# One turn of the second layer's loop for one pair of groups: scores, maximum, weighting and carries together

## The chip, the cores and the metric

The kernel runs on 1 core of one Trainium2 chip. The metric is the device time of that core in microseconds. TensorE (PE) multiplies, VectorE (DVE), ScalarE (ACT) and GpSimd (POOL) do the rest, SyncE (SP) issues most plain DMAs.

## The reference

Two graph layers run over 3125 nodes with 256 features and 50000 edges sorted by destination. The first layer is an edge network (two tanh layers, a gate from the edge attributes, a mean over the senders). The change is in the second one, an attention layer with 4 heads of 64 features:

```python
h = einsum('ni,hio->hno', x, W)
e = attn_src[:, src] + attn_dst[:, dst]
e = where(e >= 0, e, 0.2 * e) * edge_weight
e_exp = exp(e - max(e))
denom = segment_sum(e_exp, dst)
alpha = e_exp / (denom[dst] + 1e-10)
out = segment_sum(h[src] * alpha, dst)
x = layernorm(x + out)
```

## The kernel before, in words

The edges are cut into 391 blocks of 128 edges, 98 groups of 4 blocks and 49 pairs of groups (`NQ`, counted by `q`; the last pair has 7 blocks). The program first makes tables for the first layer, runs the edge network over the 98 groups (to about 1.6 ms), normalises, and writes `HT`, a table in DRAM with 260 numbers a node: the 256 features of the 4 heads and the 4 source scores. Then the second layer runs over the edges in order of destination:

- **POOL** (L1419 to L1423) gathers the rows of `HT` for each block with one indirect DMA (issue at L1407) into the ring `Hg`, which holds 12 groups (`HGR`). A group's slots are used again when VectorE has weighted the group 12 before it (`s_xb`).
- **SP** (L1300 to L1306) brings, for each pair, the destinations' remainders by broadcast into `rem` (2 slots), and stores each finished window `hist` (6 slots) to `HB` in DRAM.
- **VectorE** makes for each pair the matrix `hot` (`one_hot`, L897) and the matrices `in_window` (`window_rows`, L906). `edge_scores(q)` waits for the gathered rows of the pair and for TensorE's products of destination scores, then runs five short instructions one behind the other: add (L921), slope (L929), weight (L935), largest (L938), and the diagonal matrix `diag` of the largest (L943). `running_maximum(q)` (L950, L954) waits for TensorE's spread of that diagonal and lowers `neg_m`. `weighted_rows(g)` (L959 through `weigh`) waits for ScalarE's exponentials and writes `xb`, the rows by their weights. `carry_window(g)` (L978, L990) waits for TensorE's sums of the group and adds the window of the group before.
- **TensorE** runs `destination_scores(q)` (24 small products, L1678), `spread_maxima(q)` (L1687), and `window_sums(g)` (4 products, each recorded as two, L1698). It takes these in program order.
- **ScalarE** (L1942 to L1955) makes `drop` and the two exponentials (L1951, L1953) of a pair as soon as `neg_m` is there.

What each waits for is told by semaphores written by hand. One of them crosses from VectorE to TensorE each turn: `destination_scores(q)` waits for `s_sc` to reach `3 * (q - 1) + 1`, the first instruction of `edge_scores(q - 1)`, since both use the bank `PAD`.

The order in which VectorE takes the steps is a loop written out by hand (L1009 to L1030). It is staggered over pairs: turn `q` weights and sums pair `q`, carries pair `q - 1`, takes the maximum of pair `q + 1`, the scores of pair `q + 2`, and makes `hot` of pair `q + 3`. TensorE's loop (L1704 to L1712) has the same stagger. Every seventh pair VectorE also makes the next 14 groups' destination scores (`window_scores`, L882 to L889, six times in the loop), and once the tables for the end (`last_rows`, L995 to L1006). After the loop come `chosen` and `scale` (L1034, L1036), then the gather of the finished windows (L1473), the residual, the normalisation and the stores.

Of the kernel before, what the change touches and what calls it, by code (L numbers as in the profile page):

```python
# [17 lines left out]
def build_program(nc, xT, x, src_cols, dst_cols, src_row, dst_row, eT, w_cols,  # L18
# [85 lines left out]
    with ctx:  # L104
# [446 lines left out]
        def _(dve):  # L551
# [339 lines left out]
            def one_hot(q):  # L891

                n = edges_of_group(2 * q) + edges_of_group(2 * q + 1)
                dve.wait_ge(s_rem[q % 2], 16 * (q // 2 + 1))
                if q >= 2:
                    dve.wait_ge(s_ad, q - 1)
                dve.tensor_scalar(hot[:, q % 2, 0:n], rem[:, q % 2, 0:n], p_f[:, :], None, ALU.is_equal).then_inc(s_hot, 1)  # L897
# [13 lines left out]
            def edge_scores(q):  # L911

                blocks = blocks_of_window_pair(q)
                runs = same_rows(blocks)
                dve.wait_ge(s_hg[2 * q % HGR], group_arrivals(HGR, 2 * q))
                dve.wait_ge(s_hg[(2 * q + 1) % HGR], group_arrivals(HGR, 2 * q + 1))
                dve.wait_ge(s_ad, q + 1)
                for run in runs:
                    n, b, k = rows_of_block(run[0]), run[0], len(run)
                    j, r = b - blocks[0], b % (HGR * BLOCKS_PER_GROUP)  # L920
                    last = dve.tensor_tensor(  # L921
                        score[0:n, b:b + k, :], Hg[0:n, r:r + k, OUT:BW],
                        PAD[0:n, j * HEADS:(j + k) * HEADS].rearrange("p (k h) -> p k h", h=HEADS), ALU.add)
                last.then_inc(s_sc, 1)
                dve.wait_ge(s_sc, 3 * q + 1)
                for run in runs:
                    n, b, k = rows_of_block(run[0]), run[0], len(run)
                    v = score[0:n, b:b + k, :]
                    last = dve.scalar_tensor_tensor(v, v, NEG_SLOPE, v, ALU.mult, ALU.max)  # L929
                last.then_inc(s_sc, 1)  # L930
                dve.wait_ge(s_sc, 3 * q + 2)
                for run in runs:
                    n, b, k = rows_of_block(run[0]), run[0], len(run)
                    v = score[0:n, b:b + k, :]
                    last = dve.tensor_tensor(v, v, w_c[0:n, b:b + k].unsqueeze(2).to_broadcast([n, k, HEADS]), ALU.mult)  # L935
                last.then_inc(s_sc, 1)
                dve.wait_ge(s_sc, 3 * q + 3)
                dve.tensor_reduce(top_c[:, q:q + 1], score[:, blocks[0]:blocks[-1] + 1, :].rearrange("p b h -> p (b h)"),  # L938
                                  AX.X, ALU.max).then_inc(s_topc, 1)
                dve.wait_ge(s_topc, 2 * q + 1)  # L940
                if q >= 2:
                    dve.wait_ge(s_sp, q - 1)
                dve.tensor_scalar(diag[:, q % 2, :], ident[:, :], top_c[:, q:q + 1], None, ALU.mult).then_inc(s_topc, 1)  # L943

            def running_maximum(q):

                dve.wait_ge(s_sp, q + 1)
                if q >= 2:
                    dve.wait_ge(s_nm, q - 1)
                dve.tensor_reduce(top_g[:, q % 2:q % 2 + 1], PTOP[:, 0:P], AX.X, ALU.max).then_inc(s_mg, 1)  # L950
                dve.wait_ge(s_mg, q + 1)
                if q >= 1:
                    dve.wait_ge(s_nm, q)
                dve.scalar_tensor_tensor(neg_m[:, q + 1:q + 2], top_g[:, q % 2:q % 2 + 1], -1.0, neg_m[:, q:q + 1],  # L954
                                         ALU.mult, ALU.min).then_inc(s_nm, 1)
# [7 lines left out]
            def weighted_rows(g):  # L963

                dve.wait_ge(s_ex, g // 2 + 1)
                for run in same_rows(blocks_of_group(g)):
                    n, b, k = rows_of_block(run[0]), run[0], len(run)
                    j, i = b % (XBR * BLOCKS_PER_GROUP), b % (2 * BLOCKS_PER_GROUP)
                    r = b % (HGR * BLOCKS_PER_GROUP)
                    last = weigh(xb[0:n, j:j + k, 0:OUT], Hg[0:n, r:r + k, 0:OUT], weight_p(g // 2)[0:n, i:i + k], n, k)  # L970
                last.then_inc(s_xb, 1)

            def carry_window(g):

                q = g // 2
                if g % 2 == 0:
                    dve.wait_ge(s_drop, q + 1)
                    dve.tensor_tensor(drop_k[:, q:q + 1], drop[:, q:q + 1], keep[:, g:g + 1], ALU.mult).then_inc(s_dk, 1)  # L978
                dve.wait_ge(s_S, g + 1)
                if g >= HISTR:  # L980
                    dve.wait_ge(s_hd[g % HISTR], 16 * (g // HISTR))
                if g == 0:
                    dve.tensor_copy(hist[:, 0, 0:BW], PS[0][:, 0:BW]).then_inc(s_carry, 1)
                    return
                carried = keep[:, g:g + 1]
                if g % 2 == 0:
                    dve.wait_ge(s_dk, q + 1)
                    carried = drop_k[:, q:q + 1]
                dve.wait_ge(s_carry, g)
                dve.scalar_tensor_tensor(hist[:, g % HISTR, 0:BW], hist[:, (g - 1) % HISTR, 0:BW], carried,  # L990
                                         PS[g % 3][:, 0:BW], ALU.mult, ALU.add).then_inc(s_carry, 1)
# [14 lines left out]
                const(dve.tensor_copy(last_g[:, :, NG - 1:NG], reached[:, :, NG - 1:NG]), "last")  # L1006

            window_scores(0)
            for q in range(-3, NQ + 1):  # L1009
                if 0 <= q < NQ:  # L1010
                    weighted_rows(2 * q)
                if 0 <= q - 1:
                    carry_window(2 * q - 2)
                if 0 <= q + 1 < NQ:
                    running_maximum(q + 1)

                if 0 <= q + 2 < NQ:
                    edge_scores(q + 2)
                if 0 <= q < NQ:
                    weighted_rows(2 * q + 1)  # L1020
                if 0 <= q - 1:
                    carry_window(2 * q - 1)
                if q + 3 < NQ:
                    one_hot(q + 3)
                if 0 <= q + 1 < NQ:
                    window_rows(q + 1)
                if q >= 0 and 2 * q % ADC == 2 and 2 * q // ADC + 1 < NG // ADC:
                    window_scores(2 * q // ADC + 1)
                if q == ADC // 4:
                    last_rows()  # L1030
# [141 lines left out]
        def _(sp):  # L1172
# [121 lines left out]
            def load_remainders(q):  # L1294
                a, n = 2 * q * GE, min(2 * GE, E - 2 * q * GE)
                if q >= 2:
                    sp.wait_ge(s_hot, q - 1)
                sp.dma_start(rem[:, q % 2, 0:n], RD[0, a:a + n].partition_broadcast(P)).then_inc(s_rem[q % 2], 16)

            for q in range(-5, NQ):  # L1300
                if q + 5 < NQ:
                    load_remainders(q + 5)
                if q >= 0:
                    for g in (2 * q, 2 * q + 1):
                        sp.wait_ge(s_carry, g + 1)
                        sp.dma_start(HB[g * P:(g + 1) * P, :], hist[:, g % HISTR, :]).then_inc(s_hd[g % HISTR], 16)  # L1306
# [172 lines left out]
        def _(pe):  # L1479
# [202 lines left out]
            def spread_maxima(q):  # L1682

                pe.wait_ge(s_topc, 2 * q + 2)
                if q >= 1:
                    pe.wait_ge(s_mg, q)
                pe.matmul(PTOP[:, 0:P], ones[:, :], diag[:, q % 2, :], start=True, stop=True).then_inc(s_sp, 1)  # L1687

            def window_sums(g):

                pe.wait_ge(s_win, g // 2 + 1)
                pe.wait_ge(s_xb, g + 1)
                if g >= 3:
                    pe.wait_ge(s_carry, g - 2)
                blocks = blocks_of_group(g)
                for b in blocks:
                    n, j = rows_of_block(b), b % (XBR * BLOCKS_PER_GROUP)
                    last = pe.matmul(PS[g % 3][:, 0:BW], in_window[0:n, j, :], xb[0:n, j, :],  # L1698
                                     start=b == blocks[0], stop=b == blocks[-1])
                last.then_inc(s_S, 1)  # L1700

            pe.wait_ge(s_hc, NT)
            pe.wait_ge(s_x1c, NT)
            for q in range(-3, NQ):  # L1704
                if q >= 0:
                    window_sums(2 * q)
                if 0 <= q + 2 < NQ:
                    spread_maxima(q + 2)
                if q >= 0:
                    window_sums(2 * q + 1)  # L1710
                if q + 3 < NQ:
                    destination_scores(q + 3)  # L1712

            with if_outside(pe):
                pe.wait_ge(s_b2, B2["ones"])
# [330 lines left out]
```

## Time and profile before

| | us |
|---|---|
| median of 3 runs | 2242.31 (2242.23 to 2244.2) |
| span of the profiled execution | 2239.4 |
| start of the second layer's gathers | 1672.5 |
| first instruction of the second layer's first scores | 1684.28 |
| first instruction behind the loop (`chosen`) | 2185.59 |

The profiled execution's own time is given only by its span, which is 2.9 us under the median of the runs; that difference is what lies around the span.

Busy shares of the span: PE 87%, DVE 68%, ACT 62%, POOL 66%. In the second layer they are lower, and there the granted clock of TensorE moves between its two levels.

How to read the rows: times are microseconds from the span's start. A line of the timeline has the start, the duration, the engine, the line of the kernel and the operation with output and input; in brackets is how long the engine had been idle and what released it. A line of the groups has the busy time, the mean duration of one in ns, and behind the bar the idle time before them. Matmuls in a timeline are merged where they follow one another.

### The profile page before, as it was taken

To read this page: it belongs to the slowest core of one execution; us is meant where nothing else is said; L and a number is where in the kernel's file an instruction comes from. 1 tells how busy PE (TensorE), PEld (TensorE's weight loads), DVE (VectorE), ACT (ScalarE), POOL (GpSimd) and SP (SyncE) were. 2 spreads that over 40 slices of the span, in tenths; PEclk is the share of its full clock that TensorE was granted. 3 is DMA by queue.
4 is the path that set the end of the run, shared out by engine and by line. 5 is a ranking of instruction groups with operands and counts; after the bars stand their busy time and mean duration, and the time that the engine had idled before them with its cause. 6 is when DMAs were issued, how large, how long until landed. Compare 5 with 4: busy or idle time off the path is not lost.

```text
span 2239.4 us, 40504 instructions
## 1 busy us (share of the span) xinstructions
PE 1938.9 (87%) x12932; PEld 1717.4 (77%) x12932; DVE 1513.0 (68%) x3765; ACT 1377.2 (62%) x2758; POOL 1488.4 (66%) x1229
## 2 busy tenths in 40 slices
PE   7799999999999999999999999999664676666660
PEld 6699999999999999999999999999653455445450
DVE  6566676676666766766666667666565766666667
ACT  3488888888888888888888888888550000000012
POOL 0427677777777677777776767775427777777754
PEclk9899999999999999999999999999886767877785
DMA  7988877777777777776777777776555566656544
GB/s 241 297 221 188 201 167 171 165 161 172 158 168 171 149 167 159 154 167 152 159 165 149 166 159 154 167 153 129 119 183 142 148 160 158 161 154 162 155 125 128
DMA packets 233059, 370.78 MB, mean 166 GB/s; under 512 B 32743, under 2 KB 165825, under 8 KB 232839
## 3 DMA queue, kind: packets, MB, share of 16 engines
q0 software_dynamic: 101232, 188.20, 42.2%
q1 hardware_dynamic: 131607, 179.89, 27.5%
q8 instruction: 108, 1.77, 0.3%
q14 instruction: 112, 0.92, 0.1%
HBM read 270.57 MB, written 97.40 MB: 164 GB/s over the span
## 4 chain that ended last, share of the span: by engine, by line
PE 70%; POOL 14%; DMA 6%; issue 5%; DVE 4%; ACT 1%; SPq 0%; DVEq 0%; ACTq 0%; POOLq 0%
PE bank L1483 16%; PE bank L1482 16%; PE bank L1484 16%; POOL Hg L1407 13%; PE bank L1536 5%; PE bank L1527 5%; PE bank L1553 3%; DMA Hg<-HT,src_c 3%; PE bank L1577 2%; PE bank L1578 2%; PE bank L1589 2%; PE bank L1588 2%; DMA accA<-ystage,to_a 1%; PE bank L1654 1%; DVE xb L959 1%
## 5 line engine op out<-in xcount | busy, mean ns | idle before, releaser
L1369 POOL DMA_INDIRECT accA<-ystage,to_a x391 | 653.6, 1672 | 244.0 <-DMA accA<-ystage,to_a 113.9
L1375 POOL DMA_INDIRECT GA<-TA,src_c x391 | 424.9, 1087 | 292.7 <-issue 95.4
L1407 POOL DMA_INDIRECT Hg<-HT,src_c x391 | 378.3, 968 | 121.1 <-issue 112.8
L1482 PE MATMUL bank<-h1h,W1h 128*128 128x512 f32 x882 | 348.4, 395 | 0.0
L1484 PE MATMUL bank<-h1h,W1l 128*128 128x512 f32 x882 | 347.5, 394 | 0.0
L1483 PE MATMUL bank<-h1l,W1h 128*128 128x512 f32 x882 | 347.5, 394 | 0.0
L563 DVE TENSOR_TENSOR h2l<-h2f,h2h 128x512 fp32r<-128x512 f32 (+1 forms) x294 | 203.1, 691 | 200.8 <-ACT h2l L1769 130.5
L1698 PE MATMUL bank<-xb,in_window 128*128 128x260 f32 (+1 forms) x782 | 273.1, 509 | 58.6 <-issue 56.9
L1944 ACT ACTIVATE drop<-neg_m 128x1 f32<-128x1 f32 x49 | 14.4, 295 | 455.0 <-DVE neg_m L954 455.0
L563 DVE TENSOR_TENSOR h1l<-h1f,h1h 128x512 fp32r<-128x512 f32 x294 | 195.1, 691 | 129.5 <-ACT h1h L1769 129.5
L1698 PEld LDWEIGHTS bank<-xb,in_window 128*128 128x128 f32 (+1 forms) x782 | 190.4, 256 | 103.9 <-issue 68.4
L1769 ACT ACTIVATE mh<-mf 128x512 fp32r<-128x512 f32 x196 | 124.3, 634 | 227.5 <-DVE mf L717 227.5
L1483 PE MATMUL bank<-W2l,h2h 128*128 128x256 f32 (+1 forms) x782 | 220.5, 282 | 0.0
L1482 PE MATMUL bank<-W2h,h2h 128*128 128x256 f32 (+1 forms) x782 | 219.7, 281 | 0.4 <-DVE mf L717 0.4
L1484 PE MATMUL bank<-W2h,h2l 128*128 128x256 f32 (+1 forms) x782 | 219.9, 281 | 0.0
L1806 ACT ACTIVATE h1f<-bank 128x512 f32<-128x512 f32 (+1 forms) x392 | 206.8, 584 | 1.0 <-DVE stB L563 0.8
L1831 ACT ACTIVATE h2f<-bank,b1c 128x512 f32<-128x512 f32 x294 | 201.9, 687 | 6.7 <-PE bank L1553 1.7
L1484 PEld LDWEIGHTS bank<-h1h,W1l 128*128 128x128 f32 x882 | 166.4, 189 | 39.1
L717 DVE TENSOR_TENSOR mf<-bank,gate 128x512 f32<-128x512 f32 x196 | 135.3, 690 | 84.1 <-PE bank L1578 84.1
L1769 ACT ACTIVATE h2h<-h2f 128x512 fp32r<-128x512 f32 x294 | 185.4, 631 | 9.4
L1482 PEld LDWEIGHTS bank<-h1h,W1h 128*128 128x128 f32 x882 | 166.4, 189 | 32.1 <-issue 0.2
L1483 PEld LDWEIGHTS bank<-h1l,W1h 128*128 128x128 f32 x882 | 166.5, 189 | 30.2
(217 smaller groups left out, 4819.2 us busy)
## 6 DMA issues: line engine op xcount, KB each, us to landing
TW<-TB SPq DMA_DIRECT2D x196, 203.0 KB, 3.5
ef<-in_eT SPq DMA_DIRECT2D x97, 256.0 KB, 4.6
bcast_i<-in_src_row SPq DMA_DIRECT2D x97, 256.0 KB, 5.6
HB<-hist SPq DMA_DIRECT2D x98, 130.0 KB, 3.1
rel<-RL SPq DMA_DIRECT2D x97, 128.0 KB, 5.6
rem<-RD SPq DMA_DIRECT2D x48, 256.0 KB, 4.6
TB<-stB SPq DMA_DIRECT2D x24, 406.0 KB, 4.5
accA<-zeros SPq DMA_DIRECT2D x4, 1677.0 KB, 13.7
```

Of the source, the lines that this page charges most:

```text
L563: return dve.tensor_tensor(o, full, hi.bitcast(f32), ALU.subtract)
L717: dve.tensor_tensor(mf[0:n, q % 2, 0:k, :].rearrange("p i d -> p (i d)"), P2[0:n, 0:k * OUT], gate[0:n, q % 2, 0:k, :].rearrange("p i d -> ...
L1369: return pool.indirect_dma_start(out=table, out_offset=bass.IndirectOffsetOnAxis(ap=rows, axis=0), in_=sums, in_offset=None, compute_op=AL ...
L1375: pool.indirect_dma_start(out=GA[0:n, b % (GAR * BLOCKS_PER_GROUP), :].bitcast(f32), out_offset=None, in_=TA, in_offset=bass.IndirectOffse ...
L1407: pool.indirect_dma_start(out=Hg[0:n, slot, :], out_offset=None, in_=HT, in_offset=bass.IndirectOffsetOnAxis(ap=src_c[0:n, b:b + 1], axis= ...
L1482: pe.matmul(o, lh, rh, start=first, stop=False)
L1483: pe.matmul(o, lh, rl, start=False, stop=False)
L1484: return pe.matmul(o, ll, rh, start=False, stop=last)
L1698: last = pe.matmul(PS[g % 3][:, 0:BW], in_window[0:n, j, :], xb[0:n, j, :], start=b == blocks[0], stop=b == blocks[-1])
L1769: return act.activation(o, i, ACT.Copy)
L1806: act.activation(h1f[0:k1(c), c, 0:n], PT[u % 2][0:k1(c), 0:n], ACT.Tanh).then_inc(s_tanh1, 1)
L1831: act.activation(h2f[:, m, 0:n], PL1[u % 2][:, 0:n], ACT.Tanh, bias=b1c[:, m:m + 1]).then_inc(s_tanh2, 1)
```

## The change

VectorE's loop, SP's loop over the remainders and TensorE's loop are rewritten so that turn `q` does `edge_scores`, `running_maximum`, `weighted_rows` and `carry_window` of the same pair `q`. `one_hot(q + 2)` stands between the scores and the maximum, `window_rows(q + 1)` between the maximum and the weighting. The work inside each helper is unchanged, and no buffer changes its size.

```diff
             window_scores(0)
-            for q in range(-3, NQ + 1):
-                if 0 <= q < NQ:
-                    weighted_rows(2 * q)
-                if 0 <= q - 1:
-                    carry_window(2 * q - 2)
-                if 0 <= q + 1 < NQ:
-                    running_maximum(q + 1)
-
-                if 0 <= q + 2 < NQ:
-                    edge_scores(q + 2)
-                if 0 <= q < NQ:
-                    weighted_rows(2 * q + 1)
-                if 0 <= q - 1:
-                    carry_window(2 * q - 1)
-                if q + 3 < NQ:
-                    one_hot(q + 3)
-                if 0 <= q + 1 < NQ:
+            one_hot(0)
+            one_hot(1)
+            window_rows(0)
+            for q in range(NQ):
+                edge_scores(q)
+                if q + 2 < NQ:
+                    one_hot(q + 2)
+                running_maximum(q)
+                if q + 1 < NQ:
                     window_rows(q + 1)
-                if q >= 0 and 2 * q % ADC == 2 and 2 * q // ADC + 1 < NG // ADC:
+                weighted_rows(2 * q)
+                weighted_rows(2 * q + 1)
+                carry_window(2 * q)
+                carry_window(2 * q + 1)
+                if 2 * q % ADC == 2 and 2 * q // ADC + 1 < NG // ADC:
                     window_scores(2 * q // ADC + 1)
                 if q == ADC // 4:
                     last_rows()
...
-            for q in range(-5, NQ):
-                if q + 5 < NQ:
-                    load_remainders(q + 5)
+            for q in range(-4, NQ):
+                if q + 4 < NQ:
+                    load_remainders(q + 4)
...
-            for q in range(-3, NQ):
-                if q >= 0:
-                    window_sums(2 * q)
-                if 0 <= q + 2 < NQ:
-                    spread_maxima(q + 2)
-                if q >= 0:
-                    window_sums(2 * q + 1)
-                if q + 3 < NQ:
-                    destination_scores(q + 3)
+            destination_scores(0)
+            for q in range(NQ):
+                if q + 1 < NQ:
+                    destination_scores(q + 1)
+                spread_maxima(q)
+                window_sums(2 * q)
+                window_sums(2 * q + 1)
```

## Rows read from the trace of the kernel before

**Rows 1.** Busy time of each engine in one stretch, the second layer's loop.

```profile
core 0: us, PE busy (x) PEld busy (x) DVE busy (x) ACT busy (x) POOL busy (x), PEclk, DMA share, GB/s
1685.00:2186.00 501.00, 323.72 (x2029) 246.77 (x2029) 334.06 (x735) 38.73 (x153) 368.71 (x381) 0.77 0.60 152
```

**Rows 2.** Costliest groups of the page: the gathers and the window sums.

```profile
L1407 POOL DMA_INDIRECT Hg<-HT,src_c x391 | 378.3, 968 | 121.1 <-issue 112.8
L1698 PE MATMUL bank<-xb,in_window 128*128 128x260 f32 (+1 forms) x782 | 273.1, 509 | 58.6 <-issue 56.9
```

**Rows 3.** Line L1407 alone: shortest, median, longest in ns, first and last start.

```profile
L1407 POOL DMA_INDIRECT Hg<-HT,src_c x391: 902/953/3446, 1672.5 to 2168.8; - x196
```

**Rows 4.** Groups by line from 1715 us on: VectorE's wait for the gathered rows.

```profile
L921 DVE TENSOR_TENSOR score<-Hg,bank 128x32 f32<-128x32 f32 x44 | 8.3, 188 | 125.9 <-DMA Hg<-HT,src_c 125.9
```

**Rows 5.** Timeline at the start of the loop: scores and maximum of pair 0.

```profile
1684.28 0.19 DVE L921 TENSOR_TENSOR score<-Hg,bank 128x32 f32<-128x32 f32 x1 [8.65 <-DMA Hg<-HT,src_c]
...
1685.17 0.29 DVE L943 TENSOR_SCALAR diag<-ident,top_c 128x128 f32<-128x128 f32 x1
...
1685.51 0.80 PE L1687 MATMUL bank<-diag,ones 128*128 128x128 f32 x2 [8.85 <-DVE diag L943]
...
1686.35 0.29 DVE L950 TENSOR_REDUCE top_g<-bank 128x1 f32<-128x128 f32 x1 [0.49 <-PE bank L1687]
```

**Rows 6.** Timeline: TensorE's spread and destination scores, both at the full clock.

```profile
1973.51 0.49 PE L1687 MATMUL bank<-diag,ones 128*128 128x128 f32 x2 [4.17 <-DVE diag L943]
...
2158.58 0.87 PEld L1678 LDWEIGHTS bank<-ad_p,hot 128*128 128x128 bf16 x24
```

**Rows 7.** Timeline of one turn from weighting on, 1961.7 to 1969.4 us.

```profile
1961.71 1.21 DVE L959 TENSOR_TENSOR xb<-Hg,bank 128x1024 f32<-128x1024 f32 x1
...
1963.03 3.80 PE L1698 MATMUL bank<-xb,in_window 128*128 128x260 f32 x8 [0.38 <-issue]
...
1963.63 1.22 DVE L906 TENSOR_TENSOR in_window<-bank,rem_c 128x1024 f32<-128x1024 f32 x1
...
1964.77 1.21 DVE L959 TENSOR_TENSOR xb<-Hg,bank 128x1024 f32<-128x1024 f32 x1
...
1966.26 0.48 DVE L990 SCALAR_TENSOR_TENSOR hist<-hist,drop_k,bank 128x260 f32<-128x260 f32 x1 [0.21 <-DVE drop_k L978]
...
1966.66 0.28 DVE L950 TENSOR_REDUCE top_g<-bank 128x1 f32<-128x128 f32 x1
...
1966.98 0.16 DVE L954 SCALAR_TENSOR_TENSOR neg_m<-top_g,neg_m 128x1 f32<-128x1 f32 x1
...
1967.31 2.03 PE L1698 MATMUL bank<-xb,in_window 128*128 128x260 f32 x8
...
1967.59 0.30 ACT L1953 ACTIVATE xb<-score,neg_m 128x32 f32<-128x32 f32 x1
```

**Rows 8.** Timeline: the two window sums of two other turns.

```profile
1952.70 2.81 PE L1698 MATMUL bank<-xb,in_window 128*128 128x260 f32 x8 [0.68 <-issue]
...
1955.98 2.56 PE L1698 MATMUL bank<-xb,in_window 128*128 128x260 f32 x8
...
2155.46 3.50 PE L1698 MATMUL bank<-xb,in_window 128*128 128x260 f32 x8 [0.68 <-issue]
...
2159.41 2.00 PE L1698 MATMUL bank<-xb,in_window 128*128 128x260 f32 x8
```

**Rows 9.** Timeline: first instruction of `window_scores` and `last_rows`, and the one behind.

```profile
1718.88 1.60 DVE L882 TENSOR_TENSOR picked<-bank,in_tile 128x1400 f32<-128x1400 f32 x1
...
1722.99 1.21 DVE L959 TENSOR_TENSOR xb<-Hg,bank 128x1024 f32<-128x1024 f32 x1
...
1740.12 0.40 DVE L995 TENSOR_SCALAR n_f<-tile_row,p_f 128x25 f32<-128x25 f32 x1
...
1749.09 1.22 DVE L959 TENSOR_TENSOR xb<-Hg,bank 128x1024 f32<-128x1024 f32 x1
```

**Rows 10.** Timeline of the loop's end: the last pair's scores and the work behind.

```profile
2171.72 0.24 DVE L921 TENSOR_TENSOR score<-Hg,bank 128x24 f32<-128x24 f32 x2 [1.86 <-DMA Hg<-HT,src_c]
...
2185.59 2.71 DVE L1034 TENSOR_TENSOR chosen<-last_g,factor 128x2450 f32<-128x2450 bf16 x1
```

## The prediction, as put on record

> **What bounds the kernel now.** The change touches only the second layer's loop, so I read the busy times of that stretch first [rows 1]: in 501 us no engine is full. POOL has 369 us, DVE 334, PE 324, ACT 39. A bound must then be a pace or a chain. The groups say which: POOL's 391 gathers have 968 ns each and lose almost nothing but "issue" between them [rows 2], so POOL runs from the first to the last without a pause that another engine causes. They start from 1672.5 to 2168.8 us [rows 3]: 496.3 us for 390 steps, 1.273 us a gather, 10.2 us for a pair of 8. DVE on its side waits 125.9 us for gathered rows in the adds that open the scores [rows 4]. So **the gathers set the pace, at 10.2 us a pair, and DVE and PE have slack in every turn**. The stagger over pairs makes that slack: scores of one pair, weighting of another and carries of a third lie side by side. Behind the last landing it costs a tail: from the last pair's add at 2171.72 to `chosen` at 2185.59 is 13.9 us [rows 10].
>
> **What the change removes and adds.** No instruction is added or dropped, only the order changes. Before, DVE's results were needed one or two steps later. Now each turn is one closed chain through three engines: DVE scores, PE spread, DVE maximum, DVE weighting, PE sums of two groups, DVE carries. The next scores stand behind the last carry in DVE's order. I add the chain up from the first add (time 0).
>
> 1. From the add to `diag` are 0.89 us, and the spread can start 0.34 later [rows 5], at 1.23. But PE now has the destination scores of pair q+1 ahead of the spread, and these wait for the add of pair q (0.19 us, plus the 0.1 us that PE needs behind DVE, below): from 0.3 they take 0.87 us of weight loads [rows 6] and about 0.1 behind them, to 1.3. So the spread starts at 1.3, an extra 0.1 us. The new `one_hot(q + 2)` costs nothing: DVE would wait for the spread here in any case. Without that cover it would be about 0.4 us.
> 2. The spread takes 0.49 us at the full clock [rows 6] or 0.80 at the half [rows 5], and DVE's reduce follows 0.04 us behind (1685.51 + 0.80 to 1686.35) [rows 5]. It starts at 1.8 to 2.3; I take 2.0.
> 3. From the reduce to `neg_m` is 0.32 us, and `neg_m` takes 0.16 [rows 7]; with the step to the next instruction 0.52. `window_rows(q + 1)` stands here for 1.14 us (1963.63 to 1964.77) [rows 7]. It hides ScalarE: the second exponential ends 0.91 us behind the start of `neg_m` (1966.98 to 1967.89) [rows 7], so without it the weighting would start only some 0.4 us earlier. The first weighting takes 1.21 and PE starts 0.11 behind it (1962.92 to 1963.03) [rows 7]. PE's sums start at 2.0 + 0.52 + 1.14 + 1.21 + 0.11 = 5.0 us (4.8 at the full clock). The second weighting ends before the first sums do, so it is hidden.
> 4. **The two sums** lie back to back. This is the term with wide bounds. A group takes 2.03 us at the full clock and 3.80 at the half [rows 7], so the two take 4.0 to 7.6 us. The mean of all is 273.1 us over 98 groups, 2.79 each [rows 2], or 5.58 for two. The new order brings a break in PE's heavy work of 5.4 us in each turn, with only the scores and the spread in it. In the rows of before the sums that open a burst took 3.80, 2.81 and 3.50 us, the ones that came 3.3 to 4.3 us after that start took 2.03, 2.56 and 2.00 [rows 7, 8]. Now the second group starts when the first ends, so the clock has risen less often by then. I take 3.4 for the first and the mean 2.8 for the second, 6.2 us.
> 5. The last carry starts 0.04 us behind the sums (as the reduce behind the spread) and the next instruction 0.40 later (1966.26 to 1966.66) [rows 7]: 0.44. The first carry lies beside the second group's sums and is hidden.
>
> A turn is 5.0 + 6.2 + 0.44 = 11.6 us, against the gathers' 10.2. **DVE's chain becomes the bound**, and what was hidden in its slack is paid in full: six `window_scores` of 4.1 us (1718.88 to 1722.99) and one `last_rows` of 9.0 (1740.12 to 1749.09) [rows 9], 33.7 us.
>
> **Moved and free.** The opening `one_hot(0)`, `one_hot(1)` and `window_rows(0)` lie in the 8.65 us that DVE waits for the first rows [rows 5]. SP's load of remainders runs four pairs ahead instead of five, behind the carries of the turn before; it has about two turns until its matrix is wanted, and if that cover failed DVE would stand in `one_hot` with the maximum queued behind it. POOL's ring is freed sooner in relation to the scores (one pair is in use, not three), so the gathers run ahead and then wait for `xb`; DVE should no longer wait for rows at all. The stores of windows and everything from `chosen` on keep their order behind the last carry: zero.
>
> **The sum.** First add 1684.28, since the first landing is unchanged [rows 5]. 49 turns of 11.6 are 568.4, plus 33.7: the loop ends at 2286.4. Before, `chosen` started at 2185.59 [rows 10]. The difference is +100.8 us in the profiled execution, whose span is 2239.4: a span of 2340.2. The runs' median stands 2.9 us over the span, so **2343 us** (+4.5%).
>
> What the Trainium skill says on step 4: its page "TensorE: Matmul & The Clock Gate", section "HAM oscillation — how this bites in real kernels", tells of kernels whose bursts of products, parted by waits, start at the half clock every time. The trace agrees in part: the openers above were slow or in between, the followers mostly fast. Taken strictly, with both groups slow, it makes the second rival below.
>
> **The rivals.**
> - *The gathers stay the bound.* If PE kept the full clock, a turn would be 4.8 + 4.06 + 0.44 = 9.3 us. 49 such turns and 33.7 end at 2173.7, before the last rows could be worked off: they land at 2171.7, and one turn behind is 2181.0, 4.6 us earlier than now. That gives 2238 us, faster. For it: the tail does shrink. Against: the granted clock of the stretch is 0.77 already [rows 1] and PE's breaks grow. The point from which it decides is a turn of 9.5 us: (2185.6 - 1684.3 - 33.7) / 49. Chance 4%.
> - *Every sum at the half clock.* A turn is 5.3 + 7.6 + 0.44 = 13.3 us: 651.7 + 33.7 ends at 2369.7, +184, so 2426 us. For it: the breaks come in every turn. Against: the groups that follow an opener were mostly fast in the rows [rows 7, 8]. Chance 6%.
> - *A turn between 9.5 and 10.5 us*, with waits that overlap in a way I don't see, gives 2242 to 2290. Chance 4%, of which 1% falls within 0.2% of now.
>
> That the change does not do what it says I give no chance: each engine takes its list in order, and the waits in the chain are data.
>
> **How the numbers follow.** The forecast has 86%. Its own spread comes from step 4 and from the spread's clock: two sums of 5.3 us (under the mean of now) give a turn of 10.7 and 2299, two of 7.1 give 12.5 and 2387. The range of 2300 to 2385 leaves out about 2 in 10 with the rivals. Everything but the first rival and a corner of the third is slower by over 0.2% (4.5 us, about what a measurement of this kernel can tell from no change): faster 4%, same 1%, slower 95%.
>
> **What would show it.** Right: the scores' add no longer waits for `Hg`; POOL waits for `xb` instead and its time from first to last gather grows to nearly 600 us; the carry (L990) waits for L1698 some 4 to 6 us a turn, and PE for `diag` or `xb`; adds follow each other at 11 to 12 us. Step 1 is right if the spread starts behind the last destination product. Step 4 is wrong if the mean of L1698 falls towards 2.03 us a group or rises over 3.5. The whole is wrong if DVE still waits for gathered rows in most turns: then the gathers still bound it.

## The result

The changed kernel takes 2298.1 us (median of 4 runs, 2297.22 to 2301.32) against 2242.3 for the kernel before: a ratio of 1.025, with a 95% interval of 1.0235 to 1.0264. It is slower, as forecast, by 55.8 us where 100.8 were forecast. The range began 2 us above the measured time (2300), so the forecast was wrong in size.

The chain that ended last, from the pages of the two kernels, before and after. The first one is followed back through the whole span, the second through the second layer only (its shares add up to 25%), so PE's shares can't be compared. What can be read is that POOL, 14% of the span before, has left the chain, and PE and DVE hold it:

```profile
PE 70%; POOL 14%; DMA 6%; issue 5%; DVE 4%; ACT 1%; SPq 0%; DVEq 0%; ACTq 0%; POOLq 0%
...
PE 13%; DVE 8%; issue 4%; POOL 0%; ACT 0%; DMA 0%; ACTq 0%; DVEq 0%
```

The costliest groups, against [rows 2]. The lines have moved: the gathers are at L1403, the window sums at L1694.

```profile
L1403 POOL DMA_INDIRECT Hg<-HT,src_c x391 | 377.5, 966 | 137.1 <-issue 113.9
L1694 PE MATMUL bank<-xb,in_window 128*128 128x260 f32 (+1 forms) x782 | 273.5, 524 | 142.7 <-issue 135.7
```

The window sums cost what they cost before (273.5 us against 273.1), but PE now stands idle 142.7 us ahead of them instead of 58.6. The gathers by their own line, against [rows 3]:

```profile
L1403 POOL DMA_INDIRECT Hg<-HT,src_c x391: 902/957/3455, 1672.2 to 2183.7; - x196
...
  DVE xb L959: 20.9, 16
...
  DVE score L921: 6.8, 1
```

The second line shown is how long POOL waited for a slot of the ring (20.9 us), the third who waited for the gathers: one add, the first. Against 125.9 us in [rows 4], **VectorE waits for no gathered row any more**. Where it waits instead is in the list of waits from 1715 to 2225 us (waiting line, released by, total, times, longest):

```profile
DVE hist L990 <- PE bank L1694: 181.1, 90, 2.7
...
PE bank L1674 <- DVE score L921: 64.5, 45, 9.6
POOL Hg L1403 <- DVE xb L959: 20.9, 16, 5.3
...
DVE top_g L950 <- PE bank L1683: 10.1, 39, 0.6
```

The carries wait 181 us for the window sums, and the destination scores on PE wait for the scores' add, which stands behind those carries. One settled turn, in the timeline:

```profile
2212.39 0.18 DVE L921 TENSOR_TENSOR score<-Hg,bank 128x32 f32<-128x32 f32 x1
...
2213.28 0.28 DVE L943 TENSOR_SCALAR diag<-ident,top_c 128x128 f32<-128x128 f32 x1
...
2213.62 0.49 PE L1683 MATMUL bank<-diag,ones 128*128 128x128 f32 x2 [0.16 <-DVE diag L943]
...
2214.48 0.16 DVE L954 SCALAR_TENSOR_TENSOR neg_m<-top_g,neg_m 128x1 f32<-128x1 f32 x1
...
2215.69 2.34 DVE L959 TENSOR_TENSOR xb<-Hg,bank 128x1024 f32<-128x1024 f32 x2
...
2217.00 5.20 PE L1694 MATMUL bank<-xb,in_window 128*128 128x260 f32 x16 [2.89 <-issue]
...
2220.48 0.48 DVE L990 SCALAR_TENSOR_TENSOR hist<-hist,drop_k,bank 128x260 f32<-128x260 f32 x1 [2.39 <-PE bank L1694]
...
2222.24 0.48 DVE L990 SCALAR_TENSOR_TENSOR hist<-hist,keep,bank 128x260 f32<-128x260 f32 x1 [1.27 <-PE bank L1694]
...
2222.64 0.18 DVE L921 TENSOR_TENSOR score<-Hg,bank 128x32 f32<-128x32 f32 x1
```

The reader is to see one closed chain of 10.25 us: 4.61 from the add to the sums, 3.48 for the first sum and 1.76 from it to the second, 0.40 from the last carry to the next add. The first sum is slow and the second fast. The loop's ends, against [rows 5] and [rows 10]:

```profile
1684.01 0.19 DVE L921 TENSOR_TENSOR score<-Hg,bank 128x32 f32<-128x32 f32 x1 [6.83 <-DMA Hg<-HT,src_c]
...
2244.49 2.70 DVE L1030 TENSOR_TENSOR chosen<-last_g,factor 128x2450 f32<-128x2450 bf16 x1
```

The start is where it was and the end is 58.9 us later, which is the whole difference of the spans (2297.2 against 2239.4) but for 1.1 us. With the 33.7 us of side work (`window_scores` and `last_rows`) taken off, 49 turns took (560.5 - 33.7) / 49 = 10.75 us each.

The mean is longer than the settled turn, and the difference is most of what the chain itself costs. A turn behind side work takes 11.4 to 11.9 us: its first sum takes 3.8 us, and the second is partly slow as well (2.3 to 2.8 us behind the first). The turns behind it take 10.8, 10.5, 10.4 us and so on, down to 10.25. Had all 49 turns been settled, they would have taken 49 x 10.25 = 502 us, and the whole loop took 501.3 us before. So the settled turn as such costs nothing. The 59 us are the side work, 33.7 us, and about 24 us of turns that had not settled, the first and the last of the loop among them.

### The profile page after: what moved, and what is told of

Read it like the earlier page. It is cut to its first block and busy times, and to the rows that moved or that the text cites. A ratio compares the mean times of both kernels' runs of the same rounds, so it can differ in the third digit from the quotient of the medians.

```text
span 2297.2 us, 40504 instructions
## 1 busy us (share of the span) xinstructions
PE 1953.1 (85%) x12932; PEld 1730.3 (75%) x12932; DVE 1518.3 (66%) x3765; ACT 1378.1 (60%) x2758; POOL 1490.6 (65%) x1229
## 5 line engine op out<-in xcount | busy, mean ns | idle before, releaser
L1403 POOL DMA_INDIRECT Hg<-HT,src_c x391 | 377.5, 966 | 137.1 <-issue 113.9
L1694 PE MATMUL bank<-xb,in_window 128*128 128x260 f32 (+1 forms) x782 | 273.5, 524 | 142.7 <-issue 135.7
L1694 PEld LDWEIGHTS bank<-xb,in_window 128*128 128x128 f32 (+1 forms) x782 | 208.3, 274 | 197.8 <-issue 151.4
```

The source lines that it names most:

```text
L1403: pool.indirect_dma_start(out=Hg[0:n, slot, :], out_offset=None, in_=HT, in_offset=bass.IndirectOffsetOnAxis(ap=src_c[0:n, b:b + 1], axis= ...
```

## The experiments

Theory A: in the new order scores, spread, maximum, weighting, sums and carries are one chain through three engines, closed because the next scores stand behind the last carry, and its widest term is a first window sum that meets TensorE at the half clock. The rival: the clock, or the order, has no part in it, and either the gathers still set the pace or the chain is long whatever is moved. The runs went to several chips. On two of them the kernel before itself takes 2400.7 and 2398.6 us and not 2241, and the traces taken there show VectorE in waits for TensorE that the other chips don't show. So of the runs on these slower chips only what stands in single turns is used, and all of them but the first below were made again on another chip.

**Fewer gathers in the changed kernel** (on a slower chip).

```diff
-                for b in blocks_of_group(g):
+                for b in blocks_of_group(g)[::1 if g < HGR else 2]:
                     gather_h_rows(b, b % (HGR * BLOCKS_PER_GROUP), s_hg[g % HGR])
```

(with the count of landings that VectorE waits for cut to match).

> The changed kernel, with only every second block of a group gathered from the 13th group on (the other blocks use the rows that an earlier group left in the ring, so the second layer's sums are of other rows). POOL's pace falls from 10.2 to about 5.1 us a pair. Theory A (the gathers no longer bound the changed kernel): within 5 us of 2298. Theory B (they still set the pace): 2220 us or less.

2360.7 us. The total does not answer: in the first turn VectorE stood 21.8, 16.7 and 15.0 us in waits for TensorE, which put 60.9 us between the first two adds. The turns behind it, in which no such wait is left, do. Here is the timeline of one near the end:

```profile
2243.53 0.18 DVE L921 TENSOR_TENSOR score<-Hg,bank 128x32 f32<-128x32 f32 x1
...
2248.13 5.21 PE L1694 MATMUL bank<-xb,in_window 128*128 128x260 f32 x16 [2.88 <-issue]
...
2251.63 0.48 DVE L990 SCALAR_TENSOR_TENSOR hist<-hist,drop_k,bank 128x260 f32<-128x260 f32 x1 [2.40 <-PE bank L1694]
...
2253.78 0.18 DVE L921 TENSOR_TENSOR score<-Hg,bank 128x32 f32<-128x32 f32 x1
```

10.25 us, to the hundredth what the changed kernel takes with all its gathers. All 48 turns behind the first took 544.0 us, against 548.2 in the changed kernel (from the second add to `chosen`). The gathers do not bound it.

**Fewer gathers in the kernel before**, by the same edit.

> The kernel before, with only every second block of a group gathered from the 13th group on (the other blocks use rows that an earlier group left in the ring, so the second layer's sums are of other rows). POOL's pace falls from 10.2 to 5.1 us a pair. Theory A (before, the gathers set the pace and VectorE and TensorE had slack): the loop falls to VectorE's and TensorE's own pace in the staggered order, about 8 to 8.5 us a turn, and the time to 2130 to 2190 us. Theory B (another chain was at 10 us a turn as well): 2235 us or more.

2113.8 us, ratio 0.944 (0.9424 to 0.9455): 127 us less, more than theory A had guessed. Busy times of the stretch 1760 to 1990 us (PE, PEld, DVE, ACT, POOL, then the granted clock):

```profile
1760.00:1990.00 230.00, 171.11 (x1351) 134.75 (x1350) 216.42 (x480) 23.00 (x96) 125.79 (x132) 0.93 0.61 151
```

VectorE is busy 216 of 230 us, and its adds follow each other at 6.5 us. So the staggered order needs 6.5 us a turn, and the gathers' 10.2 us hid 3.7 us in each. The new order needs 10.75 in the mean: 4.3 us more, of which the gathers' pace hides the first 3.7. What is left (0.55 us x 49 = 27 us, nearly all of it in turns that had not settled) and the side work, which had been hidden too (33.7), make the loss.

**Idle products ahead of the sums.**

```diff
                 spread_maxima(q)
+                for _ in range(8):
+                    pe.matmul(PAD[:, 2 * P:3 * P], ident[:, :], ident[:, :], start=True, stop=True)
                 window_sums(2 * q)
```

> The changed kernel with 8 idle products (identity by identity, 128x128, into unused columns of the bank of the destination scores) between the spread and the window sums, so that TensorE's break before the sums is filled. Theory A (the loop is one chain, and its widest term is the first window sum, which finds TensorE at the half clock: 3.66 us against 1.95 for the second): both sums take about 4.1 us together instead of 5.6, a turn about 9.1 us instead of 10.7; the gathers' pace of 10.2 us a pair binds again, and the time falls to 2238 to 2255 us. Theory B (the clock is no part of it, the chain is long by its steps alone): 2298 us or a little more, since the idle products can only delay the sums.

On a slower chip: 2496.0 us against 2400.7, no better than the changed kernel's other variants with all gathers there (2464 to 2491 us). Again, on another chip:

> The same kernel as e1_filler (8 idle products ahead of the window sums), since on the chip of the first four runs the kernel before took 2400.7 us and TensorE's semaphores reached VectorE some 4 us late once a turn. On a chip where the kernel before takes about 2242 us: theory A (the first window sum finds TensorE at the half clock, and that is the widest term of the chain) 2238 to 2255 us; theory B (the clock is no part of it) 2298 us or a little more.

2232.1 us, ratio to the kernel before 0.9967 (0.9955 to 0.9978): faster than both kernels, if by little over the kernel before (8.5 us), and 6 us below the 2238 to 2255 of theory A. The timeline of a settled turn, with the idle products at L1706:

```profile
1769.60 0.18 DVE L921 TENSOR_TENSOR score<-Hg,bank 128x32 f32<-128x32 f32 x1
...
1771.15 1.95 PE L1706 MATMUL bank<-ident 128*128 128x128 f32 x16
...
1774.20 3.75 PE L1694 MATMUL bank<-xb,in_window 128*128 128x260 f32 x16 [1.10 <-issue]
...
1776.23 0.48 DVE L990 SCALAR_TENSOR_TENSOR hist<-hist,drop_k,bank 128x260 f32<-128x260 f32 x1 [0.93 <-PE bank L1694]
...
1777.99 0.48 DVE L990 SCALAR_TENSOR_TENSOR hist<-hist,keep,bank 128x260 f32<-128x260 f32 x1 [1.27 <-PE bank L1694]
```

and the busy times of the loop but for its last 13 us, in the columns of [rows 1]:

```profile
1685.00:2165.00 480.00, 354.13 (x2741) 305.03 (x2741) 331.92 (x710) 35.81 (x145) 364.78 (x379) 0.90 0.61 157
```

The sums start 4.60 us behind the add, as in the changed kernel, since the idle products end 1.10 us before them. But both sums take 3.75 us here instead of 5.20, the granted clock of the loop is 0.90 instead of 0.77 (as read in the changed kernel too, 1685 to 2244 us), and a turn in which VectorE waits for no rows and does no side work is 8.8 us (from the add to 0.40 us behind the start of the last carry). VectorE waits for gathered rows again (21.3 us in 17 adds). Nothing was taken out of the kernel; work was added to TensorE, and 66 us went. So the half clock in the first sum was what kept the chain from lying under the gathers' pace: without it a turn leaves 1.4 us to pay for the side work.

**Idle products in the kernel before**, 4 ahead of each group's sums and behind the wait for the carry, which frees their bank.

```diff
     def window_sums(g):
-                pe.wait_ge(s_win, g // 2 + 1)
-                pe.wait_ge(s_xb, g + 1)
                 if g >= 3:
                     pe.wait_ge(s_carry, g - 2)
+                for _ in range(4):
+                    pe.matmul(PS[g % 3][:, 3 * P:4 * P], ident[:, :], ident[:, :], start=True, stop=True)
+                pe.wait_ge(s_win, g // 2 + 1)
+                pe.wait_ge(s_xb, g + 1)
```

> The kernel before with idle products too: 4 ahead of each group's window sums, as many in all as in e1_filler, into unused columns of the sums' own bank. Theory A (before, the gathers set the pace, so a faster TensorE brings nothing but a shorter end of the loop): within 4 us of the kernel before. Theory B (the gain of the idle products is their own, whatever the order of the loop): 8 us or more faster, as the changed kernel with them is.

On a slower chip 2433.1 against 2398.6, ratio 1.0138. Again, on another chip:

> The same kernel as e9_filler_before. Where the kernel before takes about 2241 us: theory A (the gathers set its pace, idle products bring at most a shorter end) within 4 us of it; theory B (the idle products' gain does not depend on the order of the loop) 8 us or more faster.

2241.1 us, ratio 1.0005 (0.9995 to 1.0015). No change, with the clock of the loop at 0.85: a faster TensorE brings nothing where the gathers set the pace. The gain above belongs to the closed chain.

**Side work ahead of the first carry.**

```diff
-                carry_window(2 * q)
-                carry_window(2 * q + 1)
                 if 2 * q % ADC == 2 and 2 * q // ADC + 1 < NG // ADC:
                     window_scores(2 * q // ADC + 1)
                 if q == ADC // 4:
                     last_rows()
+                carry_window(2 * q)
+                carry_window(2 * q + 1)
```

> The changed kernel with window_scores (six times 4.1 us) and last_rows (once 9.0 us) moved from behind the last carry of their turn to ahead of its first carry, where VectorE waits about 2.4 and 1.3 us for the window sums. Theory A (VectorE's chain is the bound, so what stands behind the last carry is paid in full): some 3.7 us of each of the seven is hidden, 26 us less, 2272 us; a few us more if the shorter breaks of TensorE also raise its clock. Theory B (something else sets the pace, the side work was hidden already): within 3 us of 2298.

On a slower chip: 2491.5 us. There the reduce of the maxima, not the side work, is what is late:

```profile
2000.90 0.49 PE L1683 MATMUL bank<-diag,ones 128*128 128x128 f32 x2 [0.16 <-issue]
...
2004.87 0.29 DVE L950 TENSOR_REDUCE top_g<-bank 128x1 f32<-128x128 f32 x1 [3.63 <-remote]
```

The spread ends at 2001.4 and VectorE starts 3.5 us later; in the kernel before, on another chip, that step is 0.04 us [rows 5]. What delays it is open. Again, on another chip:

> The same kernel as e2_side_work (window_scores and last_rows ahead of the first carry of their turn), for the same reason. Where the kernel before takes about 2242 us: theory A (VectorE's chain is the bound, work behind the last carry is paid in full) 2272 us, or a few us less; theory B (the side work was hidden already) within 3 us of 2298.

2267.5 us, ratio 1.0122 (1.0105 to 1.0139): 31 us less than the changed kernel. By the two traces the seven turns with side work are 3.3 to 3.9 us shorter each, 25 us in all, near the 26 of theory A. The rest lies mostly in the turns behind them: three are 0.4 to 1.5 us shorter, while the other four still take 11.4 to 11.6 us. The side work was paid in full, as step 5 and the paragraph behind it had it.

**The carries one turn later.**

```diff
+                if q >= 1:
+                    carry_window(2 * q - 2)
+                    carry_window(2 * q - 1)
                 running_maximum(q)
...
-                carry_window(2 * q)
-                carry_window(2 * q + 1)
...
+            carry_window(NG - 2)
+            carry_window(NG - 1)
```

> The changed kernel with one part undone: the two carries of pair q stand in turn q+1, between one_hot and the maximum, so VectorE starts the next pair's scores while TensorE still sums. Theory A (what closes the chain is that the scores of q+1 stand behind the carries of q): the turn becomes the two sums plus scores' products 0.95, spread 0.5, maximum 0.4, window_rows 1.1, weighting 1.2 and the steps between, 4.4 + 5.6 = 10.0 us or less, the side work is hidden beside the sums, and the gathers bind again: 2238 to 2255 us. Theory B (the chain through maximum, weighting and sums is long enough by itself): 2280 us or more.

On a slower chip: 2485.9 us. Again, on another chip:

> The same kernel as e3_carries_later (carries of pair q in turn q+1, between one_hot and the maximum), for the same reason. Where the kernel before takes about 2242 us: theory A (the scores of q+1 behind the carries of q close the chain) 2238 to 2255 us; theory B (maximum, weighting and sums are long enough by themselves) 2280 us or more.

2238.3 us, ratio 0.9989 (0.9979 to 0.9998). Moving the carries alone to the other side of the next scores gives all of the loss back. Most turns are 9.0 to 10.9 us and the clock of the loop is 0.76, so here the slow first sum stays and the gathers hide it. That it is the gathers is read from POOL: its gathers follow each other from 1672.6 to 2166.9 us with 2.1 us of waits for slots, as back to back as in the kernel before. VectorE waits 103.2 us ahead of the scores' adds; the profile names no releaser for it, but its only other wait there, for TensorE's products of destination scores, was over 4.9 us or more before each of these adds.

**`window_rows` in the wait for the sums** (moved from behind the maximum to behind the weighting).

```diff
                 running_maximum(q)
-                if q + 1 < NQ:
-                    window_rows(q + 1)
                 weighted_rows(2 * q)
                 weighted_rows(2 * q + 1)
+                if q + 1 < NQ:
+                    window_rows(q + 1)
```

> The changed kernel with window_rows(q + 1) moved from between maximum and weighting to behind the weighting, where VectorE waits for the sums. The weighting can start when the exponentials are there, 0.94 us behind neg_m instead of 1.21: 0.27 us a turn. Theory A (every step of the chain is paid, also this one): 49 x 0.27 = 13 us faster than the changed kernel. Theory B (the settled turns of 10.24 to 10.3 us, which the changed kernel and the one with the moved side work share though their loops differ, are held by TensorE's change of clock, and what the chain gives back the slow first sum takes): less than 6 us faster.

On a slower chip 2486.3 us, ratio 1.0364. Again, on another chip:

> The same kernel as e8_rows_in_wait, again because of the chip. Where the kernel before takes about 2241 us: theory A (the 0.27 us that the chain loses in each turn are gained in full) 2285 us, ratio 1.019; theory B (turns are held at 10.24 to 10.3 us by TensorE's change of clock, the slow first sum takes what the chain gives back) 2292 us or more, ratio over 1.022.

2290.2 us, ratio 1.0223 (1.0208 to 1.0237), 8 us less than the changed kernel (6 us, if the ratios 1.0250 and 1.0223 are compared), between the 13 of theory A and the under 6 of theory B. A settled turn shows where the rest went:

```profile
2151.13 0.18 DVE L921 TENSOR_TENSOR score<-Hg,bank 128x32 f32<-128x32 f32 x1
...
2155.48 5.43 PE L1694 MATMUL bank<-xb,in_window 128*128 128x260 f32 x16 [2.63 <-issue]
...
2158.60 0.48 DVE L990 SCALAR_TENSOR_TENSOR hist<-hist,drop_k,bank 128x260 f32<-128x260 f32 x1 [0.90 <-PE bank L1694]
...
2160.95 0.48 DVE L990 SCALAR_TENSOR_TENSOR hist<-hist,keep,bank 128x260 f32<-128x260 f32 x1 [1.86 <-PE bank L1694]
...
2161.35 0.18 DVE L921 TENSOR_TENSOR score<-Hg,bank 128x32 f32<-128x32 f32 x1
```

The sums start 4.35 us behind the add instead of 4.61, a gain of 0.26, and then take 5.43 us instead of 5.20, a loss of 0.23. The turn is 10.22 against 10.25. In settled turns theory B holds: the sums take the gain back. The gain of the total lies in a few single turns: two of the seven behind side work, one that had been long in the changed kernel for another reason, and the last. Four of the others behind side work are as long as they were (11.6 to 11.9 us).

**The spread ahead of the destination scores on TensorE.**

```diff
+                spread_maxima(q)
                 if q + 1 < NQ:
                     destination_scores(q + 1)
-                spread_maxima(q)
```

> The changed kernel with spread_maxima(q) ahead of destination_scores(q + 1) on TensorE. Theory A (the recorded step 1: the 24 small products are ahead of the spread in TensorE's order and delay it by 0.1 us a turn at most; the changed kernel's trace shows TensorE idle for 0.16 to 0.21 us before diag) no change: within 4 us of the changed kernel. Theory B (the products in front of the spread are a real part of the longer turn) 10 us or more faster than the changed kernel.

On a slower chip 2464.3 us, ratio 1.0296. Again, on another chip:

> The same kernel as e6_spread_first. Where the kernel before takes about 2241 us: theory A (destination scores ahead of the spread cost next to nothing) ratio 1.023 to 1.027, as the changed kernel; theory B (they are a real part of the longer turn) ratio under 1.021.

2298.8 us, ratio 1.026 (1.0244 to 1.0277). No change, as the 0.16 us had said for which TensorE waits, behind the 24 products, until it can start the spread.

**Idle products and moved side work together.**

> The changed kernel with both: the 8 idle products ahead of the window sums, and window_scores and last_rows ahead of the first carry. With the idle products alone a turn settles at 8.8 us, under the gathers' 10.2, and the loop still pays 13 us in the turns with side work. Theory A (the gathers bound that kernel again, so more slack brings nothing but the end of the loop): within 3 us of the kernel with the idle products alone, 2228 to 2233 us where the kernel before takes 2241. Theory B (VectorE's chain still bounds it): 2215 us or less.

On a slower chip 2484.0 us, ratio 1.0353. Again, on another chip:

> The same kernel as e7_filler_and_side. Where the kernel before takes about 2241 us: theory A (with the idle products alone the gathers bound the loop again) 2228 to 2233 us; theory B (VectorE's chain still bounds it) 2215 us or less.

2234.1 us, ratio 0.9973 (0.9963 to 0.9983), with the idle products alone 0.9967. Nothing is gained by the second edit: the gathers bound both, and their last one starts at 2165.2 and 2165.4 us. The fastest version found is the changed kernel with the 8 idle products, 8.5 us under the kernel before. Of this, 4 us are won at the end of the loop: `chosen` starts at 2178.1 us, 12.7 us behind the start of the last gather, where the kernel before needs 16.8 (2168.8 to 2185.6). The gathers themselves end 3.4 us earlier.

## Why the prediction was right in kind and wrong in size

- **What bounds the kernel now.** Right. The gathers set the pace before (halving them took 127 us off), and DVE's chain sets it after (halving them left a turn at 10.25). The slack of a turn, which the prediction left without a number, was 3.7 us.
- **Step 1.** Right that the opening costs next to nothing. The 24 products take 0.68 us of weight loads, not 0.87, and end 0.16 us before the spread starts, so the "extra 0.1 us" is none.
- **Steps 2 and 3.** The sums were to start 5.0 us behind the add. In settled turns they start 4.61 behind it, in those in which the spread takes 0.8 us 4.9, in the mean 4.72. The step from the start of `neg_m` to the next instruction was taken at 0.2 us and is 0.07, and in settled turns the spread takes 0.49 us, the full clock's time. That is 0.28 us a turn, 14 us in all. The forecast had priced the cover of `window_rows` at some 0.4 us; taking it away moved the sums by 0.26.
- **Step 4, the term that failed.** "I take 3.4 for the first and the mean 2.8 for the second, 6.2 us." In the mean of 48 turns the first took 3.6 us, near its term, and the second 1.95, far under it. "The clock has risen less often by then" does not hold: in a settled turn the second sum takes 1.76 us right behind a first one of 3.48, and 1.76 is what it takes with the idle products too, where both sums are fast. The step took the second sum to be slower for following at once, and it was not. The mean of all stays at 2.79 a group, exactly the row of before [rows 2], so two sums took 5.58 us and not 6.2. That is 0.62 us a turn, 30 us in all. Had the step kept the 5.58 us that it names first, the forecast would have been 2313, inside its own range.
- **How the misses add up.** 14 and 30 us are 44. The forecast had rounded its turn from 11.64 to 11.6 us, which took 2 us back; the loop ended 41.9 us before the forecast's 2286.4. Another 1.1 us went behind the loop, and 2 us in the step from the span to the median. The text ahead of the prediction says that 2.9 us lie around the span; in every run that lists both, the time is only some 1.7 us over the span, so the rest of the 2.9 was the distance of one execution from the median.
- **Step 5 and the side work.** Right: 0.40 us from the last carry to the next add, and the side work is paid in full.
- **The rivals.** That the gathers stay the bound, if TensorE keeps the full clock, is what the idle products made true: 2238 was worked out for it, 2232 measured. The turn was put at 9.3 us and is 8.8 where it has settled. "Every sum at the half clock" did not come: the rule of the Trainium skill's page "TensorE: Matmul & The Clock Gate", section "HAM oscillation — how this bites in real kernels", that bursts parted by waits start slow, holds for the first sum of each turn; of the second sums nine in 48 took over 2.2 us, seven of them in the turn behind side work.
- **The range.** Its low end was a turn of 10.7 us and 2299, made of 5.0 us to the sums and 5.3 for them. The measured mean turn is 10.75, which lies inside it by a hair, but is made of 4.7 and 5.6; that the two agree is luck. The time fell 2 us under the range by the 3 us outside the loop. The steps ahead of the sums had no lower bound beside step 4's; with 4.6 to the sums the low end would have been 2280.
- **The signs.** The adds wait for no rows, the carries wait 4.0 us a turn, and the mean of L1698 moved neither towards 2.03 nor over 3.5: as forecast. The adds follow each other at 10.25 to 11.9 us and not at 11 to 12. The gathers take 511.5 us from first to last and not "nearly 600", and wait 20.9 us for slots. The turns of the forecast don't give 600 either: here the last gather starts 49 us before the last add, and with the forecast's last add at about 2275 us that would make some 550, an estimate.

## What to carry to other kernels

Before closing a loop over three engines into one chain, add up the chain and compare it with the pace that another queue sets anyway: here 6.5 us of staggered work were free under 10.2 us of gathers, and 10.75 us of chained work with 33.7 us of side work behind it were not. It took moving one step, the carries, to the other side of the next scores to get all of it back. Where a row of before gives the mean of a term whose clock moves, keep the mean unless a row shows a trend, and give the bounds to every step of the sum, not to the widest alone.

## What was not expected of the hardware

The changed kernel's turns fall from 11.9 us behind a long one to 10.25 and stay near it. With the chain 0.26 us shorter the turn was 10.22 and the sums 0.23 us longer, and with fewer gathers on another chip it was 10.25 again. In that shorter chain the nine turns ahead of the last took 10.21 to 10.23 us and their sums 5.43 each, while the time from their start to the first carry fell from 3.17 to 3.00 us and that from the first carry to the second rose from 2.30 to 2.47. So the loop and TensorE's change of clock seem to hold each other at a period; that is a reading of these turns, and no run here tests it by itself. A saving of 0.26 us in the chain brought a settled turn 0.03 us, while the idle products, with which the granted clock rose to 0.90, brought it to 8.8 us. They lengthen TensorE's own work and took 66 us off this kernel, but nothing off the kernel whose bound they did not touch.
